# Twelve gather steps of layer 1 and six of layer 2 of a graph network, copied row by row by SyncE beside the steps before them

## What is computed

```python
# layer 1 (L0_gnn): the near end is x[src], the far end x[dst]
h    = relu(x[src] @ W1[:128] + x[dst] @ W1[128:] + b1)
mask = sigmoid(h @ W2 + b2)
agg  = segment_sum(mask / (segment_sum(mask, src)[src] + 1e-9) * x[dst], src)
x    = layernorm(x + relu((0.5 * x + 0.5 * agg) @ Wl + bl))
# layer 2 (L1_gnn)
h    = concat(x[src], x[dst], edge_attr) @ W1 + b1
msg  = (relu(layernorm(h) * ln_g + ln_b) @ W2 + b2) * sigmoid(edge_attr @ gate_w + gate_b)
agg  = segment_sum(msg, dst)
x    = layernorm(x + gru(agg, x))
```

## Time and profile before

| | |
|---|---|
| median of 3 runs | 4732.17 us (4730.84 to 7622.93) |
| the profiled execution | 4731.59 us, of which its span is 4729.8 us |
| busy | PE 71%, PEld 62%, DVE 76%, ACT 50%, POOL 67% |
| the chain that ended last | POOL 32% of the span, issue 11% |
| layer 1 | groups from about 480 to 2560 us |
| layer 2 | groups from about 2590 to 4670 us |

### The profile page before, as it was taken

The page is one execution under the profiler, slowest core; times in us unless marked ns, Lnnn a source line. Parts: engine busy times, 40 slices in busy tenths (PEclk is TensorE's granted clock), DMA queues, the critical chain, the costliest instruction groups (busy, mean ns, idle before and its releaser), DMA issues. The chain is left out here.

```text
span 4729.8 us, 106816 instructions
## 1 busy us (share of the span) xinstructions
PE 3365.4 (71%) x20905; PEld 2948.7 (62%) x20906; DVE 3587.4 (76%) x14554; ACT 2370.7 (50%) x6569; POOL 3180.9 (67%) x3367
## 2 busy tenths in 40 slices
PE   6551566666666666666664778888888888888887
PEld 4441555555555565555553667777777777777775
DVE  8995777777777777777776778777777777777775
ACT  2210323333444333443332666777777777777775
POOL 0003777777777777777774777777777777777773
PEclk9665777777777778777786989999999999999997
DMA  3112445555555555555553444444444444444442
GB/s 115 47 29 73 144 135 146 147 148 148 148 147 147 147 146 147 148 148 148 148 148 109 115 105 115 114 115 113 116 116 115 115 115 114 115 115 115 114 114 53
DMA packets 597448, 574.46 MB, mean 121 GB/s; under 512 B 320589, under 2 KB 462931, under 8 KB 597308
## 3 DMA queue, kind: packets, MB, share of 16 engines
q0 software_dynamic: 133632, 328.29, 25.9%
q1 hardware_dynamic: 463676, 244.70, 19.0%
HBM read 535.82 MB, written 43.09 MB: 122 GB/s over the span
## 5 line engine op out<-in xcount | busy, mean ns | idle before, releaser
L1779 POOL DMA_INDIRECT front_rows<-c,gather_index x1660 | 1578.9, 951 | 505.8 <-issue 505.4
L743 POOL DMA_INDIRECT front_rows<-bx,gather_index x832 | 789.6, 949 | 256.8 <-issue 250.7
L743 POOL DMA_INDIRECT bxrows<-bx,gather_index x828 | 782.9, 945 | 252.5 <-issue 251.6
L1812 PE MATMUL pre<-w1e,efT 128*128 128x129 f32 x3328 | 681.0, 288 | 156.0 <-DVE h L2020 145.2
L1286 PE MATMUL pre<-near,hotT 128*128 x3328 | 555.5, 336 | 225.8 <-DVE h L1439 184.6
L1462 DVE TENSOR_TENSOR acc<-acc,scattered 128x129 f32 x1664 | 465.7, 280 | 328.1 <-ACT mask L1369 324.2
L1286 PEld LDWEIGHTS pre<-near,hotT 128*128 128x128 f32 x3328 | 520.5, 245 | 272.9 <-issue 268.6
L1814 PE MATMUL pre<-near,hotT 128*128 x3328 | 665.7, 283 | 0.0
L1812 PEld LDWEIGHTS pre<-w1e,efT 128*128 128x128 f32 x3328 | 529.9, 201 | 181.8 <-DVE h L2020 151.1
L1465 DVE SCALAR_TENSOR_TENSOR hotw<-row_bank,places,mask 128x128 f32<-128x128 f32 x1664 | 571.0, 344 | 2.4 <-ACT mask L1369 2.2
L1362 ACT ACTIVATE sig<-logit,b 128x8 f32<-128x8 f32 x208 | 62.6, 301 | 971.2 <-DVE h L1446 965.3
(11 more groups left out here) (299 smaller groups left out, 6238.3 us busy)
## 6 DMA issues: line engine op xcount, KB each, us to landing
spread<-place_rows SPq DMA_DIRECT2D x416, 256.0 KB, 3.7
ef<-in_edge_attr SPq DMA_DIRECT2D x1664, 32.0 KB
front_rows<-c,gather_index POOLq DMA_INDIRECT x1660
front_rows<-bx,gather_index POOLq DMA_INDIRECT x832
bxrows<-bx,gather_index POOLq DMA_INDIRECT x828
x_turned<-x1T SPq DMA_DIRECT2D x98, 64.0 KB
g_xT<-x_turned SPq DMA_DIRECT2D x98, 64.0 KB
x_a<-in_x SPq DMA_DIRECT2D x97, 64.0 KB
```

What stands on the lines that cost most here:

```text
L743: nc.gpsimd.indirect_dma_start(out=there[:, k, 0:2 * D], out_offset=None, in_=s.bx[:, :], in_offset=bass.IndirectOffsetOnAxis(ap=s.index[: ...
L1779: pool.indirect_dma_start(out=crows[q][:, k, 0:D], out_offset=None, in_=s.c[:, :], in_offset=bass.IndirectOffsetOnAxis(ap=s.index[:, g * G ...
L1812: nc.tensor.matmul(pre[:, bank, at:at + W], efT[par][:, k // 2, :], w1e2[:, k % 2, :], start=True, stop=False)
```

## The change

SyncE takes over 18 of the gather steps. In layer 1 steps 0 to 7 of group 142 and 0 to 3 of group 200, in layer 2 steps 0 to 5 of group 198 are no longer gathered by GpSimd. In their place SyncE copies their 1536 + 768 rows one by one from the table into a table of their own in DRAM (`staged0`, `staged1`): behind its slot of each group from 4 to 195, 8 rows in layer 1 and 4 rows in layer 2. For this it loads the 8 or 4 row numbers into registers and issues a DMA for each row, whose source address and, in the hardware loops, target address come from registers. When the group comes up, SyncE loads the staged rows with one plain DMA for each step (`fill`). VectorE waits for these on a semaphore `filled` and for 16 less on `rows_in` for each step left out. The row numbers come from `index`: in layer 1 through DRAM into one partition at the start, in layer 2 straight into a fourth row of `step_rows1`.

```diff
+ROWS0, ROWS1 = 8, 4
+BY_SP0, BY_SP1 = {142: 8, 200: 4}, {198: 6}
+SPLIT0, FIRST0, LAST0 = 33, 36, 49
+LAST1 = 49
+
+def stage_rows(nc, sp, picked, g, each, table, there, done):
+    rows = load_values(nc, mybir.EngineType.SP, picked[0:1, bass.ds((g - R) * each, each)], N - 1)
+    for i in range(each):
+        sp.dma_start(there[bass.ds((g - R) * each + i, 1), :], table[bass.ds(rows[i], 1), :]).then_inc(done, 16)
 
 def gather_rows(nc, s, there, g, done):
-    for k in range(gathered_steps(g)):
+    for k in range(BY_SP0.get(g, 0), gathered_steps(g)):
...
@@ layer 1, SyncE @@
+                def stage(g, q, done):
+                    stage_rows(nc, sp, picked, g, ROWS0, s.bx, s.staged0, done[q])
+
+                def fill(g, at, done, each):
+                    n = BY_SP0[g]
+                    sp.wait_ge(scattered, 3 * (g - R) + 3)
+                    for q in range(R):
+                        sp.wait_ge(done[q], 16 * each)
+                    from_rows = s.staged0[at:at + n * P, :].rearrange("(p k) d -> p k d", k=n)
+                    for k in range(n):
+                        sp.dma_start(bx[g % R][:, k, 0:2 * D], from_rows[:, k, :]).then_inc(filled[g], 16)
+
+                def body(o, done):
+                    for q in range(R):
+                        steps(o * R + q, q, o)
+                        nodes(o * R + q, q, o)
+                        if done:
+                            stage(o * R + q, q, done)
...
@@ layer 1, VectorE @@
+                        if isinstance(g, int) and g - 1 in BY_SP0:
+                            dve.wait_ge(filled[g - 1], 16 * BY_SP0[g - 1])
...
@@ layer 2, SyncE @@
+                    def stage(g, q):
+                        stage_rows(nc, sp, picked, g, ROWS1, s.c, s.staged1, staged[q])
...
+                    with sp.Fori(JOINED, LAST1) as o:
+                        for q in range(R):
+                            steps(o * R + q, q, o, True)
+                            nodes(o * R + q, q, o)
+                            stage(o * R + q, q)
+                    for g in range(LAST1 * R, LAST + 1):
+                        steps(g, g % R, g // R, True)
+                        nodes(g, g % R, g // R)
+                        if g in BY_SP1:
+                            n = BY_SP1[g]
+                            sp.wait_ge(pre_used, 3 * (g - R) + 3)
+                            for q in range(R):
+                                sp.wait_ge(staged[q], 16 * (LAST1 - 1) * ROWS1)
+                            from_rows = s.staged1.rearrange("(p k) d -> p k d", k=n)
+                            for k in range(n):
+                                sp.dma_start(crows[g % R][:, k, 0:D], from_rows[:, k, :]).then_inc(filled[g], 16)
...
@@ layer 2, GpSimd @@
-                    for k in range(gathered_steps(g)):
+                    for k in range(BY_SP1.get(g, 0), gathered_steps(g)):
```

More of the change, by code:

```diff
@@ L734, with taken @@
 EARLY = 2
+ROWS0, ROWS1 = 8, 4
+BY_SP0, BY_SP1 = {142: 8, 200: 4}, {198: 6}
+SPLIT0, FIRST0, LAST0 = 33, 36, 49
+LAST1 = 49
+STAGED0, STAGED1 = sum(BY_SP0.values()) * P, sum(BY_SP1.values()) * P
+assert (SPLIT0 - 1) * R * ROWS0 == BY_SP0[142] * P and (LAST0 - 1) * R * ROWS0 == STAGED0
+assert (LAST1 - 1) * R * ROWS1 == STAGED1
+def taken(by_sp, q, upto=GROUPS):
+    return sum(n for g, n in by_sp.items() if g % R == q and g <= upto)
+def stage_rows(nc, sp, picked, g, each, table, there, done):
+    rows = load_values(nc, mybir.EngineType.SP, picked[0:1, bass.ds((g - R) * each, each)], N - 1)
+    for i in range(each):
+        sp.dma_start(there[bass.ds((g - R) * each + i, 1), :], table[bass.ds(rows[i], 1), :]).then_inc(done, 16)
 def gathered_steps(g):
@@ L1128, in layer0_stage @@
         acc = s.acc
+        picked, pick_out, pick_in = sb("picked0", [1, STAGED0], I32), sem("pick_out"), sem("pick_in")
+        staged_first = [sem(f"staged_first{q}") for q in range(R)]
+        staged_last = [sem(f"staged_last{q}") for q in range(R)]
+        filled = {g: sem(f"filled{g}") for g in BY_SP0}
         wl, bias = sb("wl", [P, D], F32), sb("bias_rows", [P, 2, D], F32)
@@ L1192, in _ @@
                 load_spread(0, 0)
+                at = 0
+                for g, n in BY_SP0.items():
+                    there = s.pick0[:, at * P:(at + n) * P].rearrange("a (p k) -> (a p) k", k=n)
+                    sp.dma_start(there, s.index[:, g * G:g * G + n]).then_inc(pick_out, 16)
+                    at += n
                 sp.dma_start(tile_of[:, :], s.tile_of[0][:, :]).then_inc(steps_in, 16)
@@ L1217, in nodes @@
                         for p in range(R):
-                            sp.wait_ge(rows_in[p], 16 * STEPS // R - (16 * NEVER if p == R - 1 else 0))
+                            sp.wait_ge(rows_in[p], 16 * (sum(gathered_steps(n) for n in range(p, GROUPS, R)) - taken(BY_SP0, p)))
                         sp.dma_start(s.index[:, :], s.index1[:, :]).then_inc(s.index_in, 16)
@@ L1249, in nodes @@
                         store_rows(i, s.c, c_of(i), c_out)
-                loop_slots(sp, steps, nodes, LAST)
+                def stage(g, q, done):
[14 more added lines that the diff above has]
+                            stage(o * R + q, q, done)
+                body(0, None)
+                with sp.Fori(1, 4) as o:
+                    for q in range(R):
+                        steps(o * R + q, q, o)
+                        stage(o * R + q, q, staged_first)
+                for o in range(4, FILL):
+                    body(o, staged_first)
+                with sp.Fori(FILL, SPLIT0) as o:
+                    body(o, staged_first)
+                with sp.Fori(SPLIT0, FIRST0) as o:
+                    body(o, staged_last)
+                fill(142, 0, staged_first, (SPLIT0 - 1) * ROWS0)
+                with sp.Fori(FIRST0, LAST0) as o:
+                    body(o, staged_last)
+                body(LAST0, None)
+                steps(50 * R, 0, 50)
+                nodes(50 * R, 0, 50)
+                fill(200, BY_SP0[142] * P, staged_last, (LAST0 - SPLIT0) * ROWS0)
+                for g in range(50 * R + 1, LAST + 1):
+                    steps(g, g % R, g // R)
+                    nodes(g, g % R, g // R)
                 sp.wait_ge(x1_out, 32 * PAIRS)
@@ L1554, in nodes, with body @@
                         dve.tensor_tensor(ka[:, :, :], half[:, :, :], has_edges[:, :, :], ALU.mult).then_inc(factors, 1)
-                loop_slots(dve, steps, nodes, LAST)
+                def body(o, upto=0):
+                    for q in range(R):
+                        steps(o * R + q, q, o, upto)
+                        nodes(o * R + q, q, o)
+                body(0)
+                with dve.Fori(1, 4) as o:
+                    for q in range(R):
+                        steps(o * R + q, q, o)
+                for o in range(4, FILL):
+                    body(o)
+                at = FILL
+                for n in BY_SP0:
+                    with dve.Fori(at, n // R) as o:
+                        body(o, n - 1)
+                    at = (n + 1) // R + 1
+                    for o in range(n // R, at):
+                        body(o)
+                for g in range(at * R, LAST + 1):
+                    steps(g, g % R, g // R)
+                    nodes(g, g % R, g // R)
 BEHIND = 4
@@ L1562, with joined_slots @@
 assert FIRST_JOINED * G // TILES >= 3
-def joined_slots(engine, steps, nodes, last, at_joined=None):
+def joined_slots(engine, steps, nodes, last, at_joined=None, rolled=BODIES):
     def body(o):
@@ L1579, in joined_slots @@
         at_joined()
-    with engine.Fori(JOINED, BODIES) as o:
+    with engine.Fori(JOINED, rolled) as o:
         for q in range(R):
@@ L1583, in joined_slots @@
             nodes(o * R + q, q, o)
-    for g in range(GROUPS, last + 1):
+    for g in range(rolled * R, last + 1):
         steps(g, g % R, g // R, True)
@@ L1659, in layer1_stage @@
         acc = s.acc
+        picked, pick_in = step_rows.bitcast(I32)[3:4, 0:STAGED1], sem("pick1_in")
+        staged = [sem(f"staged1_{q}") for q in range(R)]
+        filled = {g: sem(f"filled1_{g}") for g in BY_SP1}
         slot = [(k // 3, (k % 3) * W) for k in range(G)]
@@ L2009, in steps @@
                         p1 = (q - 1) % R
-                        dve.wait_ge(rows_in[p1], o * (16 * G) + (0 if q == 0 else 16 * G) - (16 * NEVER if never(g) else 0))
+                        if isinstance(g, int) and g - 1 in BY_SP1:
+                            dve.wait_ge(filled[g - 1], 16 * BY_SP1[g - 1])
+                        less = 16 * taken(BY_SP1, p1, g - 1) if isinstance(g, int) else 0
+                        dve.wait_ge(rows_in[p1], o * (16 * G) + (0 if q == 0 else 16 * G) - less
+                                    - (16 * NEVER if never(g) else 0))
                         if used(g, 3):
```

41 lines of the change are left out of this document (36 added, 5 removed).

## The result

The changed kernel takes 5100.49 us in the median of 4 runs (5096.85 to 5135.9), the kernel before 4732.34 us beside it (4 runs, one of which took 7622.93 us and is not in the ratio). The ratio is 1.080, with a 95% interval of 1.074 to 1.086: **8.0% slower**, where 4.8% was forecast and 5070 us was the range's end.

A forecast was written before the change was run, and what follows sets the result against it. GpSimd's gathers were taken to bound the kernel, with SyncE becoming layer 2's bound after the change: 4731.6 - 15 (layer 1) + 243 (layer 2: 246 + 10 - 13) = 4960 us, 4.8% slower; range 4860 to 5070 us.

The forecast's parts named there:

- layer 2, groups 39 to 196: Layer 2's loop over passes 10 to 48: SyncE needs 46.3 us against GpSimd's 40.0, 39 x 6.3 = 246 us more.
- layer 2, up to group 39: Layer 2's early passes: staging costs 23 us, SyncE's lead absorbs about 13, leaving +10 us.
- layer 2, from group 196 to the end: Layer 2 after staging ends: twelve groups run at about 8.7 instead of 10.0 us, less some 2 for `fill`: -13 us.
- the price of a row: SyncE's cost of one staged row: 0.59 us, with 0.333 for the issue; low end 0.44, high end 0.70.
- The load of four row numbers: SyncE in layer 2: loading four row numbers takes 0.86 us, 0.99 with register work and gaps.
- the 13 us that SyncE's lead was to absorb: Layer 2's early passes: SyncE issues features ahead of need, so about 13 of 23 us delay nobody.
- Add 10 for the early passes: Layer 2: 10 us added to the range's ends of 4866 and 4991 us, reckoned from row prices 0.44 and 0.64.
- it fits, by 2.3 us a pass: Layer 1: with staging SyncE works 37.6 of each 39.9 us pass, so GpSimd stays the bound.
- The sign named for being wrong: One of three such signs: layer 1's pass longer than 40 us.
- GpSimd stays the bound, and its 12 gathers are gained: Layer 1: 12 gathers removed at 1.25 us each save 15 us.
- the copies of the row numbers: Start of layer 1: two copies hold SyncE some 5 us while it would wait anyhow.
- rival 3: SyncE becomes layer 1's bound too, from 0.66 us a row: 5018 us, at 0.70 a row 5107 us; chance 12%.

The follow-up runs named there:

- e7: Kernel before plus layer 2's part only, its 4 rows a group copied into SBUF instead of DRAM, steps filled from first 768 rows of `c`: 4856.24 us, ratio 1.022.
- e11: Kernel before plus layer 1's part only, its 12 steps taken from groups 200 and 201 so no main loop is split: 4763.04 us, ratio 1.003.
- e4: Kernel before plus layer 1's part of the change only, layer 2 as before: 4769.3 us, ratio 1.005.
- e10: Kernel before plus layer 1's part only, with 4 rows a group and 6 steps, all of group 200, no loop split: 4730.27 us, ratio 0.9985.
- e12: Changed kernel with 221 empty wait instructions ahead of VectorE's second layer 1 loop: 5106.11 us, ratio 1.072.
- e8: Kernel before plus layer 2's part only, no row staged, the six steps filled from the first 768 rows of `c`: 4725.4 us, ratio 0.9995.
- e1: Changed kernel with 40 instructions of empty waits ahead of VectorE's second layer 1 loop: 5108.68 us, ratio 1.078.
- e6: Kernel before plus layer 2's part only, with 2 rows a group and 3 steps: 4826.76 us, ratio 1.019.
- e2: Kernel before with only VectorE's layer 1 loop split in two, pass 35 written out between: 4816.64 us, ratio 1.012.
- e9: Kernel before with VectorE's layer 1 loop split and 222 empty wait instructions ahead of the second loop: 4738.27 us, ratio 0.9995.
- e5: Kernel before with VectorE's layer 1 loop split and 128 empty wait instructions ahead of the second loop: 4809.21 us, ratio 1.013.

## Why the prediction was wrong

Right were the direction and the mechanism of layer 2: SyncE works 32.9 us of a pass (47.9 - 4 x 3.67 gives 33.2), it takes the chain from GpSimd, the wait of the earlier trace rows goes, GpSimd waits for the addition, the clock sinks and TensorE, busy 332 of 400 us, doesn't decide. The sizes were off, and one mechanism was missing. Forecast +228 us on 4731.6, measured +372 in the profiled executions:

| term | forecast | measured |
|---|---|---|
| layer 2, groups 39 to 196 | +246 | +311.5 |
| layer 2, up to group 39 | +10 | +28.6 |
| layer 2, from group 196 to the end | -13 | -13.4 |
| layer 1, gathers gone | -15 | -3.5 |
| layer 1, start and first loop | 0 | +7.0 |
| layer 1, VectorE's second loop | none | +41.6 |

The forecast is short by 144 us: 65.5 in the main stretch of layer 2, 41.6 by the second loop, 18.6 in the early groups of layer 2, 11.5 by gathers that bring little and 7.0 ahead of the second loop. With the 311.5 us foreseen and nothing else changed the sum would have been 5025 us, inside the range; it takes the others to leave it.

**The step that failed first is the price of a row**, "I take 0.333, the row nearest to 16 pieces in kind". The register work around the issue was right, 0.257 against 0.263 us measured; the issue takes 0.520, so a row 0.78 to 0.79 instead of 0.59, and even the high end of 0.70 was too low. The nearest row in kind was in the trace of before, and I didn't use it: seven copies from DRAM to DRAM, which issued in 0.50 us.

```profile
L500 SPq DMA_DIRECT2D bx<-in_x x7: 497/503/681, 58.2 to 351.5; - x7
```

With 0.503 a row is 0.76. I had ordered the rows by their number of pieces; e7 shows that the destination matters more. The load of four row numbers went the other way, 0.54 with its register work and gaps against 0.99: I took its price from 16-bit values, and these are 32-bit (eight of them load in 0.536 us, eight 16-bit ones in 1.65). The two misses cancel in part: a slot takes 3.67 instead of 3.35, so 39 x 4 x 0.32 = 50 us of the 66 that are missing there, and 33.2 for 32.9 gives 12 more. The early groups' 28.6 us I did not take apart: their rows cost 0.70 us where 0.525 was taken, and the 13 us that SyncE's lead was to absorb hardly show. The range's "Add 10 for the early passes" counts these passes twice, since the 3 us taken off before it are 10 - 13 already; it moves the ends by 10 us.

**Layer 1, "it fits, by 2.3 us a pass"**: it does, without those 2.3 us. Slots of 7.13 against 6.51 use them up, and what is over costs nothing that shows (e11). The sign named for being wrong, a pass of layer 1 longer than 40 us, did come: 43.2 us from group 144 on, but by VectorE's loop. **"GpSimd stays the bound, and its 12 gathers are gained"** is the second failed step. After, e4, e10 and e11 have the gathers away and take 103.9 to 105.6 us from group 196 to 207 instead of 108.3, 2.7 to 4.4 us less. In e10 and e11 all of these gathers are missing in the last groups, and there a group costs 9.3 us even with rows that are ready: a saved 1.25 us is worth 1.25 only until the next engine's pace, and VectorE's 7.6 us of busy time a group leave out its wait for the mask (e11). What the eight gathers of group 142 bring by themselves no run shows, since either the stalling loop (after, e4) or the empty waits (e12) stand behind them. In layer 2 the same saving came out at 7 us (e8). At the start of layer 1 the copies of the row numbers were to cost nothing; group 4 comes at 519.7 to 522.5 us in the early traces that have them (after, e1, e4, e10, e11) and at 517.4 to 518.6 in those that don't (before, e6, e8).

**VectorE's second loop** was in the diff and in no term. I costed SyncE's new loops by their instructions and VectorE's not at all, as it issues nothing new. e2, e9 and e12 show it: 13 back branches of some 3.7 us in after, 48 us, of which 41.6 are lost by group 196. That rival 3's 5107 us came near the result is luck: its 62 us in layer 1 were to come from SyncE's pace, which e11 and e12 refute, and its slot of 3.79 us in layer 2 came near 3.67 with a row too cheap and row numbers too dear.

Nothing beats the kernel before by more than these runs can tell. e8, which stages nothing, is the bound for layer 2's part, 7 us; a step costs SyncE 128 x 0.79 = 101 us and spares GpSimd one gather of 1.25.

## What to carry to other kernels

Price a new DMA by the row that shares its source and its destination before one that shares its size; here DRAM to DRAM issued in 0.52 us and DRAM to one SBUF partition in 0.23. When a queue with no busy share becomes the bearer of work, add up its pass from durations and compare it with the waits it has; that term was right within 0.3 us. When a diff cuts a hardware loop in two, look behind the back branches of the new loop: the same instructions at another place in memory can stall at each of them. The profile calls it "issue", and the packets of the instruction queue give it away. And before a saved microsecond is counted in full, add to the next engine's busy time what it waits for its own partners.

## What the runs showed of the hardware

- A back branch of VectorE's loop of 316 instructions has a gap of 0.3 us or of 2.8 to 4.9 us behind it, by the loop's place: bad at 34, 35, 75 and 162 instructions (modulo 256) from a good one, good again at 768. Where it is bad, five packets of 8 KB a pass run on the instruction queue. Loops of 269, 246 and 217 instructions showed at most 0.3 us at every place they had here.
- SyncE's loads into registers: eight 32-bit values 0.536 us, four 0.30, but two 0.47; eight 16-bit values 1.65.
- A DMA of one row of 512 bytes issued in 0.520 us from DRAM to DRAM (0.513 with a fixed target), as did one of 1 KB (0.521), and in 0.231 us into an SBUF partition.
- An empty wait on a semaphore long reached took VectorE 0.09 to 0.10 us: groups 140 to 144 take 61.5 us with 222 of them (e9) and 52.6 with 128 (e5), against 40.3 before. Most of it is caught up where VectorE has room: e9's early executions end some 8 us late (4735 to 4739 against 4726 to 4735).
